# Expert regions that run through a whole layer: 35 slot pairs in four phases instead of two groups of 19, with the loads, scatters and preparation rescheduled

## The reference, cut to what matters

```python
x = x + 0.5 * ffn(layernorm(x), ...)      # top 2 of E = 4 experts
x = x + attn(layernorm(x), ...)           # 16 heads, cumulative state
x = x + 0.5 * ffn(layernorm(x), ...)
# ffn(h):
g = softmax(layer_norm(h) @ router_w.T); top2_w, top2_idx = top_k(g, 2)   # weights normalised
hid = relu(layer_norm(h @ w1[e]))         # D 256 -> H 512
out = sum over the two experts of weight * (hid @ w2[e])
return layer_norm(out)
```

## Time and profile before

| | us |
|---|---|
| median of 3 runs | 1112.97 (1111.69 to 1113.45) |
| profiled execution | 1112.76 |
| its span | 1110.9 |
| TensorE busy in the span | 864.4 |
| VectorE / ScalarE / GpSimd busy | 723.6 / 500.8 / 564.9 |
| mean granted clock of TensorE | 0.902 |

### The profile page before, as it was taken

The page is one execution under the profiler, slowest core; times in us unless marked ns, Lnnn a source line. Parts: engine busy times, 40 slices in busy tenths (PEclk is TensorE's granted clock), DMA queues, the critical chain, the costliest instruction groups (busy, mean ns, idle before and its releaser), DMA issues.

```text
span 1110.9 us, 26786 instructions
## 1 busy us (share of the span) xinstructions
PE 864.4 (78%) x8660; PEld 664.8 (60%) x8660; DVE 723.6 (65%) x2096; ACT 500.8 (45%) x950; POOL 564.9 (51%) x631
## 2 busy tenths in 40 slices
PE   1534499988999797898888988974899989999600
PEld 1423278766888675556555545652787778888500
DVE  5647777576678673578778766553674775777336
ACT  2542266432444343664665655521565334444311
POOL 4046233562356451876886567463226443555373
PEclk9957599998999898998998999985999999999855
DMA  8042564674467431111112112124536567666343
GB/s 303 7 165 106 135 169 120 160 184 117 112 156 166 115 101 29 40 40 48 46 43 58 29 41 69 43 93 114 155 108 173 144 160 162 158 156 158 126 125 102
DMA packets 191146, 126.06 MB, mean 113 GB/s; under 512 B 126373, under 2 KB 180905, under 8 KB 190633
## 3 DMA queue, kind: packets, MB, share of 16 engines
q1 hardware_dynamic: 177746, 89.72, 30.7%
q0 software_dynamic: 12288, 33.57, 10.4%
q10 hardware_dynamic: 984, 1.07, 0.3%
HBM read 50.89 MB, written 47.19 MB: 88 GB/s over the span
## 4 chain that ended last, share of the span: by engine, by line
PE 45%; DVE 16%; issue 12%; POOL 9%; ACT 6%; DMA 5%; SPq 4%; another core or an unknown queue 3%; ACTq 0%; DVEq 0%; POOLq 0%
PE banks L1906 4%; PE banks L1891 4%; PE banks L1893 4%; PE banks L1892 4%; PE banks L1907 4%; PE banks L1908 4%; PE banks L1991 3%; SPq L518 3%; POOL slots_in L605 3%; PE banks L1993 2%; PE banks L1867 2%; PE banks L1992 2%; PE banks L1868 2%; PE banks L2106 2%
## 5 line engine op out<-in xcount | busy, mean ns | idle before, releaser
L613 POOL TENSOR_TENSOR stds<-vare,expo 128x4 f32<-128x4 f32 x76 | 80.5, 1060 | 205.7 <-DVE vare L920 205.4
L1891 PE MATMUL banks<-area,w1h 128*128 128x256 f16 x608 | 168.8, 278 | 1.0 <-DVE area L934 1.0
L1893 PE MATMUL banks<-area,w1l 128*128 128x256 f16 x608 | 168.4, 277 | 0.7 <-issue 0.7
L1892 PE MATMUL banks<-area,w1h 128*128 128x256 f16 x608 | 168.7, 277 | 0.0
L1906 PE MATMUL banks<-w2all,area 128*128 x608 | 166.2, 273 | 2.7 <-DMA w2all<-w_kept 1.9
L1908 PE MATMUL banks<-w2all,area 128*128 x608 | 165.8, 273 | 0.9 <-issue 0.8
L1907 PE MATMUL banks<-w2all,area 128*128 x608 | 165.8, 273 | 0.5 <-issue 0.5
L934 DVE SCALAR_TENSOR_TENSOR area<-banks,area 128x512 f16<-128x512 f32 x152 | 104.3, 686 | 74.6 <-ACT area L1449 59.7
L1449 ACT ACTIVATE area<-banks 128x512 f16<-128x512 f32 x152 | 89.5, 589 | 123.4 <-PE banks L1893 101.6
L605 POOL DMA_INDIRECT slots_in<-area,spos x96 | 103.5, 1079 | 78.2 <-DVE spos L855 52.5
L737 POOL TENSOR_TENSOR area<-area 128x512 f16<-128x512 f32 x64 | 81.7, 1286 | 92.9 <-ACT area L1660 92.7
(11 more groups left out here) (278 smaller groups left out, 2215.9 us busy)
## 6 DMA issues: line engine op xcount, KB each, us to landing
area<-slots_in SPq DMA_DIRECT2D x76, 256.0 KB
slots_out<-area SPq DMA_DIRECT2D x152, 128.0 KB
X<-in_L_attn_x_dram SPq DMA_DIRECT2D x8, 512.0 KB, 5.8
slots_in<-zrow SPq DMA_DIRECT2D x16, 256.0 KB
area<-area SPq DMA_DIRECT2D x256, 16.0 KB
out_dram<-X SPq DMA_DIRECT2D x32, 128.0 KB
area<-slots_in SPq DMA_TRANSPOSE x152
area<-in_L_ffn_w_dram SPq DMA_DIRECT2D x4, 512.0 KB, 12.5
```

Of the source, the lines that this page charges most:

```text
L1891: pe.matmul(o, w1h[c][m][:, bass.ds(e, 1), :], a[:, c], start=(c == 0), stop=False)
L1892: pe.matmul(o, w1h[c][m][:, bass.ds(e, 1), :], a[:, KC + c], start=False, stop=False)
L1893: last = pe.matmul(o, w1l[c][m][:, bass.ds(e, 1), :], a[:, c], start=False, stop=(c == KC - 1))
```

## The change

One tensor `slots_in` (and one `slots_out`) holds a whole layer: the expert regions run on through both groups, so that only NT + E - 1 = 35 pairs are needed for 32 tiles. The table of pairs is made in four phases, each when one more octet has been placed: pairs 0 to 4, 5 to 12, 13 to 15 and 16 to 34 (`PHASE`). A phase takes pairs that are already full; the last takes what is left. `tables` becomes longer (prefix sums over up to 8 segments) and runs four times a layer instead of twice, `positions` compares each slot with 24 block bounds. The loads of a phase's pairs are issued at the earliest in the steps of `LOAD_AT` = (-5, 0, 10, 13). The second group's tiles are routed two a step in nine steps from one step ahead of the loop (`OCTET_AT` = 3, 7) and their `row_T` and `router` are moved one step later and behind the step's matmuls; `std_T` moves ahead of `layer1(j, 0)` and `prefix` to the end of the step. Scatters and gathers beyond the first of a step or chunk wait for another engine's progress (`b_Rl`, `a_y`, in the preparation `r_hT`, `p_mx`, `p_gl`). Gathers of the first group follow `LEFT` in steps 20 to 32. In `weights` the order on all engines changes, the last part of it (w2's low halves) moves into `mixture`, and a second `quad_norm` and two tiles' rows come ahead of the loop. `mixture(1)` loads `w2` back once all scatters have landed; its first five pairs wait only for the first octet.

```diff
-    NJ = GT + E - 1
-    NP = 2 * NJ
+    NP = NT + E - 1
+    PHASE = (0, TO - E + 1, GT - E + 1, GT, NP)
+    SEGS = (1, 1, 2, 2)
+    SEG0 = (0, 1, 2, 4, 6)
+    NB = SEG0[-1] * E
+    K1 = GT + E - 1
...
-        ROUTED = (0, 2, 3, 5, 6, 8, 10, 11, 13, 14, 16)
-        OCTET_AT = (5, 10)
+        ROUTED = (0, 2, 4, 6, 8, 10, 12, 14, 16)
+        OCTET_AT = (3, 7)
+        MOVED = 2
+        LEFT = (2, 1, 1, 2, 1, 1, 2, 1, 1, 1, 1, 1, 1)
+        LOAD_AT = (-AHEAD, 0, 10, 13)
...
-        ROW_AT = 8
-        MOVES = (2, 3)
+        ROW_AT = 7
+        MOVES = (1, 2)
...
             def load_slots(p):
+                f, j = p // NP, p % NP
+                if j in PHASE:
+                    phase = PHASE.index(j)
+                    sp.wait_ge(r_tab, NO * f + phase + 1)
+                    sp.wait_ge(sc_h[phase % GO], 32 * TO * (2 * f + phase // GO + 1))
+                    if phase == NO - 1:
+                        sp.wait_ge(sc_p, 16 * E * (f + 1) + 16)
...
+            def load_at(j):
+                for at, lo in reversed(tuple(zip(LOAD_AT, PHASE))):
+                    if j >= lo:
+                        return max(j - AHEAD, at)
...
-                for p in range(p0, p1):
-                    if p > p0:
-                        store_slots(p - 1, 0)
-                        store_slots(p - 1, 1)
-                    if p + AHEAD < p1:
-                        load_slots(p + AHEAD)
+                    for o in range(GO):
+                        sp.wait_ge(sc_h[o], 32 * TO * 3)
                     sp.wait_ge(m_w2, 16)
                     sp.dma_start(w2flat, w2_kept).then_inc(m_w2, 16)
+                for j in range(NP):
+                    if j > 0:
+                        store_slots(p0 + j - 1)
+                    if j in (11, 12):
+                        for e in range(2):
+                            pad(f, 2 * (j - 11) + e)
+                    for i in range(NP):
+                        if load_at(i) == j:
+                            load_slots(p0 + i)
...
+                for t in range(GT - TB):
+                    if t < TO:
+                        pool.wait_ge(r_hT, t + TO)
+                    if t == TO + 1:
+                        pool.wait_ge(p_mx, 3)
+                    if t > TO + 1:
+                        pool.wait_ge(p_gl, t - TO + 1)
                     scatter(GT * G + t)
...
+                    for t in moves(j):
+                        if t > moves(j)[0]:
+                            pool.wait_ge(b_Rl, 2 * p + 1)
                         scatter(GT * (G + 1) + t)
...
                     for i in moves_in(c):
+                        if i > moves_in(c)[0]:
+                            pool.wait_ge(a_y, c + 1)
                         scatter(i)
...
+            def positions(G):      # on VectorE
+                passed = part(576, [GT, NB])
+                for k in range(2):
+                    step(dve.tensor_tensor(passed, rows_in[:, G % 2, k]..., block_at..., ALU.is_ge))
+                    step(dve.tensor_tensor(passed, passed, jump..., ALU.mult))
+                    step(dve.tensor_reduce(es[:, :, k], passed, AX.X, ALU.add))
...
+                for j in range(NP):      # on TensorE
+                    p = p0 + j
+                    turn = routed(j - 1)
+                    if j + 2 < NP:
+                        e[p + 2] = expert(p + 2)
+                        grams(p + 2, e[p + 2])
+                    if j + 1 < NP:
+                        std_T(p + 1, i1 + started(j - 2))
+                    layer1(p, 0, e[p])
+                    for t in turn[:1]:
+                        pe.wait_ge(b_sdr, p + 2)
+                        row_T(i1 + t)
+                    if j > 0:
+                        layer2(p - 1, 0, e[p - 1])
+                    for t in turn[1:2]:
+                        row_T(i1 + t)
+                    layer1(p, 1, e[p])
+                    for t in turn[2:]:
+                        row_T(i1 + t)
+                    if j > 0:
+                        layer2(p - 1, 1, e[p - 1])
+                    if octet(j, 1) is not None:
+                        prefix(O1 + octet(j, 1))
+                    for t in turn:
+                        router(i1 + t)
...
```

More of the change, by code:

```diff
@@ L354, in octet, with leaves @@
             return OCTET_AT.index(j - d) if j - d in OCTET_AT else None
+        def leaves(j):
+            k = j - K1 - 1
+            return range(sum(LEFT[:k]), sum(LEFT[:k + 1])) if 0 <= k < len(LEFT) else ()
         def beside(i):
@@ L1188, in mixture @@
                     relu_low(p, 1)
[L1189 removed]
+                    if octet(j, 1) is not None:
                         place(O1 + octet(j, 1))
+                    for t in tiles[2:]:
+                        row_low(i0 + GT + t)
+                    if octet(j, 0) is not None:
+                        logits(O1 + octet(j, 0))
                     if f == 0:
[L1192 to L1193 removed]
+                        ahead(j)
+                    if j + 3 < NP:
                         twice_low(p + 3)
```

631 lines of the change are left out of this document (341 added, 290 removed).

## The result

The changed kernel takes 1118.9 us (median of 12; the kernel before 1112.0 beside it), a ratio of 1.0082, interval 1.0062 to 1.0101. The prediction said 1092. Its profiled span is 1116.6 us against 1110.9.

What follows compares the result with a forecast made beforehand. TensorE was taken to set the pace inside a layer. From the profiled 1112.8 us, 1112.8 - 38.2 + 32 - 15 + 15 - 11 - 4 = 1091.6, say 1092 us; range 1054 to 1112.

Steps and rivals of the forecast that it cites:

- Six pairs fewer: Both layers' loops: 38 pairs become 35, each removed one a bare pair of 6.4 us; -38.2 us, bounds 36 to 44.
- Longer tables and positions on VectorE: Loops and attention: longer `tables` and `positions` delay steps, partly covered by idle time and double buffer; +15 us, between +3 and +49.
- the prediction's signs: Expected in the profile after: among others, steps 5, 9 and 17 a few us longer, with `std_T` waiting for VectorE.
- The positions: VectorE's loop steps: `positions` with two `add_offset` delays step 17 by 2.5 us and step 19 by 1.
- VectorE becomes the bound: Rival: tables between the two `relu_low` stand in TensorE's path whole, 49 us instead of 15; 1126 us, chance 0.13.
- Late loads: `grams` of pairs 13 and 16, both layers: four gaps, 8.8 us each with clock; +35, net +32, bounds 11 and 45.
- Scatters paced: Attention's last chunk (7 us) and both loops (5 and 3): held-back scatters spare TensorE halts; -15 us, between nothing and -20.
- Preparation: Ahead of the first loop: tables, rows and gram parts fill VectorE's idle gaps; net -11 us, between 0 and -18.
- start of the second layer: Second layer's first loads go out during attention, w2 at once; VectorE's work remains a wait; -4 us, between 0 and -9.
- its rule that short gaps are free: TensorE's clock: gaps of 5.0 and 5.2 us are followed by 0.50, one of 3.0 us stays at 1.00.

Runs made afterwards that it cites:

- d4: e1 with the steps that gather two tiles moved to 22, 25 and 28 from 20, 23 and 26; 1098.6 us, 0.9903 of the kernel before.
- g1: e1 with five steps a layer that gather two tiles instead of three; 1118.9 us, 1.0032 of the kernel before.
- e5: e1 with tables and positions last in VectorE's step and token sums and outputs behind `std_parts`; 1105.6 us, 0.9907 of the kernel before.
- d2: Kernel before plus 26 dependent VectorE instructions (5.2 us) mid-step in steps 5, 9 and 33 of each layer; 1140.7 us, 1.0280.
- d5: Kernel before plus the same 5.2 us chains as d2, but at the end of VectorE's step; 1134.2 us, 1.0224.
- e1: Changed kernel with loads of phases 2 and 3 and the rows of zeros one step earlier; 1101.9 us, 0.9876 of before; on a later chip 1101.2, 0.9939.
- n1: Changed kernel without the waits that hold back a step's second scatter or gather in loops and attention; 1121.6 us, 1.0062 of the kernel before.
- g2: e1 with eight steps a layer that gather two tiles, in a row; 1123.3 us, 1.0043 of the kernel before.

## Why the prediction was wrong

**Where the error lies.** Take the time of each interval from scaling to scaling above a bare step of 6.5 us, by stretches of the loop, in us (the two numbers are before and after):

| intervals | first layer | second layer | change, both | predicted |
|---|---|---|---|---|
| 0 to 12: routing, tables, loads | 12.6 to 38.5 | 15.7 to 35.5 | +45.7 | +32 |
| 13 to 19: boundary, offsets, positions | 16.0 to 17.5 | 3.3 to 4.4 | +2.6 | +4 |
| 20 to the end: gathers | 8.1 to 16.2 | -5.6 to 4.9 | +18.6 | 0 |

With six bare pairs of 6.5 gone, -39, that gives the +28 of the two loops; predicted were -2.

**The step that failed** first, the one with the larger error, is in "Six pairs fewer": that gathering spreads "over the pairs that are left, so what goes is the bare pair", since the pairs taken out "carry no tile of their own". The bare pair is right (quiet steps take 6.5 us, three in a row in the second layer). But 16 tiles in 13 steps means three steps with two, and a second tile costs 3 us (18.6 / 6) where the first is free. The text never priced a double gather. d4 and g1 show that the doubling is the cause: the long steps move with it, and four more doubles add 20 us to this stretch. How a second tile costs so much is read from the timelines alone: its landing holds ScalarE's `relu_high` (953.36 in the kernel after), and its sum of 1.3 us stands ahead of `std_parts`. e5 took the sums away and left the landing, and the stretch stayed at 20.3 us against 20.5; so the landing is the likelier part, but no run moved `first_weighted`. Nor does a landing by itself cost anything: in the kernel before ScalarE waits for one 15 times in the second group (39.9 us in all), and TensorE does not stand.

**The second** is in "Longer tables and positions on VectorE": "a table of 5.5 us between the two `relu_low` delays the next step by about 2 us". It took VectorE's mean idle time in a step, 2.2 us, and the double buffer of `relu_low` as cover. The 2.2 joins the busy share of the first group to the step length of the second; each by itself, rows 2 give 2.5 and 1.7. d2 shows 5.2 us for such a chain, not 2, and d5 4.1 where it stands at the step's end, so that neither of the two places tried has the cover that was counted on. The wait first shows at `std_T` of the next step (as the prediction's signs had it), which needs `std_parts`, and that stands behind the added work. In the kernel before, `std_parts` ends 4.8 us ahead of `std_T` in a bare step (931.03 to 935.86), but only 0.9 to 2.7 us where one token's sums are in the step (0.9 from 941.48 to 942.39). In the kernel after `std_T` stands waiting for it, with positions (927.04) as with two tokens (958.41). If `std_parts` is out already, as in d5, the next thing behind the chain is waited for instead, 2.2 us for `variances`. Clock comes on top in most cases, which this term left out and that of the late loads did not. In the intervals 0 to 12, beside 35 for the loads, -3 had been put down for tables and pacing together (+5, -8); with the loads at 35, it was +11. How that splits into the dearer tables and the pacing that brought nothing was not measured. The positions were right: intervals 16 and 18 are 9.0, 2.5 above bare each.

The rival "VectorE becomes the bound" had the price, 1126, and nearly the mechanism, at a chance of 0.13; it named the tables alone and the `relu_low` pair as the place.

**Late loads**: right in place, number and size. Four gaps of 5.8 to 6.3 us, 24.4 together; the two intervals with them in the second layer, 16.2 and 14.3, are 9.7 and 7.8 above a bare step, 8.8 in the mean, as predicted. That the mean agrees to a tenth is luck: the gaps are 0.4 us shorter than the 6.5 of the sum and the clock behind them costs some 1.6, not 2.3, which makes 7.7; the rest of these intervals is other work of the step. e1 takes the first one away, from 16.2 to 7.8 and 6.2.

**Scatters paced**: wrong for the loops; without the waits nothing changes there that can be measured. The long interval of the kernel before in that place (11, 13.2 us in the second layer) is 6.1 and 6.2 in the kernel after and in n1, so that the waits did not remove it. In attention the last chunk falls from 15.3 to 9.5 us, near the 7 predicted, but n1 has 12.4 without any wait: only 3 of it are the pacing. That ten scatters now stand in several chunks is then the likelier cause of the rest, which was only argued. The prediction weighed the Trainium skill ("Runtime: NRT & Kernel Launch", Instruction fetch mechanics), where fetching across a block is mostly hidden; no run here tells what holds the engines during scatters, so that this stays open.

**Preparation** (-11.2), **start of the second layer** (-4.8): the nets are right; the terms that they were added up from were not measured one by one. The start's remaining wait is the one named, for VectorE ahead of the first `grams` and `layer1`. That is 2.6 us in the waits of that stretch of the kernel after:

```profile
PE banks L2010 <- DVE var L1026: 2.6, 2, 1.9
```

The errors add up: +18.6 for the gathers, +13.7 in intervals 0 to 12, -1.4 for positions and boundary, and -3.7 in small ones elsewhere, some 27 us in all, from 1092 to 1119.

**What stays open.** No run gathers one tile a step with 35 pairs, so that the 18.6 us are not shown to go with the doubles. Whether the landing of the second tile or its sums set the price was not separated. Why g2's eight doubles cost no more than g1's five is not explained; the releaser of its waits isn't named. Why e5, with `std_T`'s waits nearly gone, is no faster than e1, is explained only in part: other waits for VectorE appear, and d5 shows that a chain costs 4.1 us even where it holds nothing at once. Whether a table split over several steps would be free was not tried.

## What to carry to other kernels

Slack is not the engine's mean idle time in a step. Read it in the timeline, for every result that stands behind the new work, as the distance from its end to the instruction that needs it, before a chain is added and again when the consumer is moved forward. Moving the chain only changes which result is late, and a wait that gets shorter proves nothing until the loop does. Look at the engines that feed the late one, too: here ScalarE stood waiting for a landing ahead of the work that mattered. When tiles are packed into fewer steps, price the step that now has two, not the steps that vanish. Price each gap with the clock behind it, as a range where the gap is short. Work that is taken out of the busy engine comes back as waits if the helper engine's work per step grows at the same time.

## What was not expected of the hardware

Short gaps of TensorE do not cost a fixed amount of clock. In the kernel after, a gap of 2.7 us (955.7 to 958.4) is followed by 3.6 us at a mean of 0.53; in e1 a gap of 2.6 us in the same step is followed by 3.5 us at 1.00, and in the kernel after one of 2.3 us (1002.5) and one of 2.7 us (172.6) are too. In d5 a gap of 2.2 us is followed by 4.4 us at 0.65. The late loads' gaps of 5.8 to 6.3 us all have 0.50 to 0.56 behind them. The prediction took one gap of 3.0 us with 1.00 in its window, and that gap had 1.00 behind it too; its rule that short gaps are free held there and failed for others of the same length. What decides between the two is not shown by these runs. The fall also can't be read from the window of the gap, which shows 1.00 ahead of 0.58 as it does ahead of 1.00: read the one behind it.
